# Batch by batch: the norms, transposes and copies ahead of the second mixture of experts

## The reference

```python
x = x + jnp.tanh(g_xattn[2]) * _L2_xattn_ref(_layernorm(x, axis=-1), ctx_2048, ...)
x = x + jnp.tanh(g_ffn[2]) * _L2_ffn_ref(_layernorm(x, axis=-1), ...)

def _L2_ffn_ref(x, router_logits, gating_einsum, linear, per_expert_scale, router_scale):
    var = jnp.mean(jnp.square(x.astype(jnp.float32)), axis=-1, keepdims=True)
    router_input = x * jax.lax.rsqrt(var + 1e-06) * root_size * router_scale
    logits = jnp.einsum('gsd,de->gse', router_input, router_logits)      # 8 experts
    _, choices = jax.lax.approx_max_k(logits, k=2)
    # softmax weights of the two chosen; each expert: gelu(x w_gate) * (x w_up), then its linear
```

## Time and profile before

| | us |
|---|---|
| median of 3 runs | 1482.22 |
| lowest, highest | 1480.7, 1485.71 |
| the profiled execution, its time | 1479.47 |
| the profiled execution, its span | 1477.8 |
| PE busy | 1335.5 (90%) |
| DVE busy | 1031.1 (70%) |
| ACT busy | 795.1 (54%) |
| POOL busy | 668.1 (45%) |
| mean granted clock of PE | 0.963 |

### The profile page before, as it was taken

One profiled execution on the slowest core, in us unless ns is written; L12 is line 12 of the kernel. 1 busy time (PEld: TensorE's weight loads), 2 busy tenths in 40 slices (PEclk: granted clock), 3 DMA queues, 4 the chain that ended last, 5 costly groups with the idle time before them and its releaser, 6 DMA issues.

```text
span 1477.8 us, 23050 instructions
## 1 busy us (share of the span) xinstructions
PE 1335.5 (90%) x7138; PEld 1093.5 (74%) x7138; DVE 1031.1 (70%) x2191; ACT 795.1 (54%) x1978; POOL 668.1 (45%) x675
## 2 busy tenths in 40 slices
PE   5987999998899999977899889999989899999994
PEld 3545888886487877766788567888877788888884
DVE  7786556555687777657754757878787877786654
ACT  6744222222566666653222467767777677787342
POOL 1010454543343434324632145556557676766443
PEclk9997999998999999997999999999999999999997
DMA  6221545562200000010110199000120000105283
GB/s 217 93 93 52 173 160 176 161 181 61 79 8 23 8 16 1 1 43 15 43 43 28 43 253 293 7 1 15 30 94 29 30 30 29 58 17 193 76 285 112
DMA packets 66705, 120.80 MB, mean 82 GB/s; under 512 B 6644, under 2 KB 35976, under 8 KB 65579
## 3 DMA queue, kind: packets, MB, share of 16 engines
q1 hardware_dynamic: 64347, 115.33, 24.8%
q0 software_dynamic: 2256, 4.22, 0.8%
HBM read 82.53 MB, written 38.96 MB: 82 GB/s over the span
## 4 chain that ended last, share of the span: by engine, by line
PE 61%; DVE 17%; issue 7%; ACT 6%; DMA 5%; POOL 4%; SPq 1%; POOLq 0%; DVEq 0%; ACTq 0%
PE ps L1479 8%; PE ps L1452 8%; PE ps L1430 7%; PE ps L1351 6%; PE ps L1497 6%; PE ps L1295 5%; PE ps L1462 4%; PE ps L1157 4%; PE ps L1441 3%; DMA w<-in_l1f_w 3%; PE ps L1365 3%; PE ps L1311 2%; POOL urs L910 2%; DVE usum L2847 2%; DVE nmax L2872 1%
## 5 line engine op out<-in xcount | busy, mean ns | idle before, releaser
L917 POOL TENSOR_TENSOR probs<-probs,prec 128x512 f32<-128x512 f32 x192 | 202.1, 1053 | 324.2 <-DVE prec L2879 323.9
L2068 ACT ACTIVATE probs<-ps,nmax 128x256 f32<-128x256 f32 x384 | 178.6, 471 | 217.9 <-DVE nmax L2872 217.6
L1479 PE MATMUL ps<-probs_t,v_tok 128*128 128x256 f32 x768 | 200.7, 385 | 0.2 <-ACT ob L2087 0.2
L1452 PE MATMUL ps<-k_feat,q_feat 128*128 128x256 f32 x768 | 198.6, 381 | 1.9 <-ACT q_feat L2059 1.9
L910 POOL TENSOR_TENSOR urs<-uve,neg_half 128x4 f32<-128x4 f32 x136 | 136.9, 1007 | 56.4 <-DVE uve L2848 45.8
L2872 DVE TENSOR_REDUCE nmax<-ps 128x2 f32<-128x512 f32 x192 | 131.6, 686 | 31.4 <-PE ps L1452 28.4
L1452 PEld LDWEIGHTS ps<-k_feat,q_feat 128*128 128x128 f32 x768 | 137.4, 191 | 16.0 <-issue 2.7
L1462 PEld LDWEIGHTS ps<-ident,probs 128*128 128x128 f32 x768 | 93.8, 142 | 64.8 <-issue 36.6
L1479 PEld LDWEIGHTS ps<-probs_t,v_tok 128*128 128x128 f32 x768 | 133.0, 193 | 10.8 <-ACT probs_t L2077 0.4
L1462 PE MATMUL ps<-ident,probs 128*128 128x128 f32 x768 | 117.7, 276 | 20.9 <-ACT probs_t L2077 20.5
L2077 ACT ACTIVATE probs_t<-ps 128x512 f32<-128x512 f32 x192 | 115.1, 599 | 3.2 <-PE ps L1462 3.2
(11 more groups left out here) (405 smaller groups left out, 3626.4 us busy)
## 6 DMA issues: line engine op xcount, KB each, us to landing
rows_in<-zero_rows SPq DMA_DIRECT2D x3, 5160.0 KB, 40.9
tile_w<-in_l3f_w SPq DMA_DIRECT2D x21, 385.5 KB, 7.3
w<-in_l1f_w SPq DMA_DIRECT2D x24, 256.0 KB, 6.6
spread_w<-we_dram SPq DMA_DIRECT2D x16, 384.0 KB, 3.8
kv_cross<-kv_out SPq DMA_DIRECT2D x20, 256.0 KB, 2.2
kv_first<-kv_out SPq DMA_DIRECT2D x16, 256.0 KB, 2.0
spread_w<-we_dram SPq DMA_DIRECT2D x16, 256.0 KB, 3.9
w<-in_l2f_w SPq DMA_DIRECT2D x8, 512.0 KB
```

The source lines that it names most:

```text
L917: pool.tensor_tensor(p3, p3, spread(prec[g % 3][:, :], [P, TB, S]), ALU.mult)\
L1452: mm = pe.matmul(ps[g % 2][:, j * S:(j + 1) * S], q_feat[:, h, j * P:(j + 1) * P], k_feat[:, kv, :], start=True, stop=True)
L1479: mm = pe.matmul(ps[6][:, 0:S], v_tok[:, tb, kv * P:(kv + 1) * P], probs_t[g % 2][:, tb, :], start=tb == 0, stop=tb == TB - 1)
L2068: ins = act_e.activation(probs[g % 4][:, j, :], ps[g % 2][:, j * S:(j + 1) * S], ACT.Exp, bias=nmax[g % 3][:, j:j + 1], accum_out=psums[g ...
```

## The change

The work on the normalised x is cut into batches, and that for batches 0, 1 and 2 is put into the hooks of the last slots of `l2x`:

- DVE: statistics in slots 54, 55, 56, the shift in 57, 58, 59, the rests `h_lo` in 66, 67, 68.
- POOL: three roots of 2 columns in slot 57.
- ACT: the centred and scaled `h_tok` in slots 58, 60, 61, the copy to `h_feat` in 63, 64, 65, the rounded copy `h_hi` in 65, 66, 67.
- PE: four identity products per batch in slots 62, 63, 64.

Only batch 3 is done after the attention, in the same steps. `h_tok` is now made by ACT, from shift and scale, and no longer by DVE. The router's mean square isn't taken from moments of `h_tok`, but worked out from variance and scale of x (`rstd`² · variance), and its root (L896 in the changed kernel) stands on POOL behind the first weight split. PE does the logits of the first three batches, then eight products with the identity whose result nobody reads (`keep_clock`), and then batch 3. ACT's one copy of the output weights is cut into four, in units 2 to 5 of the experts.

```diff
@@ POOL @@
-            run(attention(L2X))
-            ln_scale()
-            ln_scale()
-            split_weights(L2F, lambda: low_output(wsets[1]["o"]))
+            def scales_second(t):
+                if t == 57:
+                    part_scales(3)
+            run(attention(L2X, scales_second))
+            part_scales(1)
+            split_weights(L2F, lambda: low_output(wsets[1]["o"]), root_mean_square)
...
                     first(0, 0)
+                    first_split()
                     first(0, 1)
...
+            def root_mean_square():
+                n_ln[0] += B
+                pool.wait_ge(ln_var, n_ln[0])
+                pool.tensor_tensor(rrec[:, :], var_eps[:, :], neg_half[:, 0:NT], ALU.pow).then_inc(ln_rstd, B)
@@ PE @@
-            run(attention(L2X, begin_late(FIRST_LN, h_tok)))
-            turn(h_tok, h_ready, (1, 2))
-            feat_ready()
-            logits(wg2, 8)
+            def toward_l2f(t):
+                first_late(t)
+                if t in (62, 63, 64):
+                    b = t - 62
...
+                    turn_part(SECOND_LN, b, h_tok, quantised, (SECOND_LN - 1) * B + b + 1, ps[2 + b % 2])
+            run(attention(L2X, toward_l2f))
+            pe.wait_ge(part_out, SECOND_LN * B + 3)
+            logits(wg2, 8, 0, 3 * TB)
+            keep_clock(8, 6)
+            turn_part(SECOND_LN, 3, h_tok, quantised, SECOND_LN * B, ps[5])
+            pe.wait_ge(part_out, SECOND_LN * B + 4)
+            logits(wg2, 8, 3 * TB, NT)
@@ ACT @@
                 late(t)
+                if t in (58, 60, 61):
+                    centre_part(SECOND_LN, (58, 60, 61).index(t), h_tok)
+                if t in (63, 64, 65):
+                    second_copy(t - 63, ps[2 + (t - 63) % 2])
+                if t in (65, 66, 67):
...
+                    second_high(b, part(h_feat, b))
...
-            copy_turned(h_feat, h_hi)
+            centre_part(SECOND_LN, 3, h_tok)
+            second_copy(3, ps[5])
+            second_high(3, two(ps[5]))
             router(8, ACT.Exp, 2)
-            act_e.wait_ge(layer_done, 5)
-            act_e.wait_ge(lw["wo_in"], 16)
-            act_e.activation(w_high["o"][:, :, :], wsets[1]["o"][:, :, :], ACT.Copy)\
-                .then_inc(lw["wo_hi"], 1)
-            experts(L2F)
+            def high_output(u):
...
+                if 2 <= u < 6:
+                    heads = slice(4 * (u - 2), 4 * (u - 1))
+                    copied = act_e.activation(w_high["o"][:, heads, :], wsets[1]["o"][:, heads, :], ACT.Copy)
+                    if u == 5:
+                        copied.then_inc(lw["wo_hi"], 1)
+            experts(L2F, high_output)
@@ DVE @@
-                if t == 62:
-                    variance(x_tok, 0)
+                if t in (54, 55, 56):
+                    part_moments(SECOND_LN, t - 54)
+                if t in (57, 58, 59):
+                    part_shift(SECOND_LN, t - 57)
+                if t in (66, 67, 68):
+                    second_low(t - 66)
...
-            layernorm(x_tok, 1)
-            v.wait_ge(turned_out, 4 * 1)
-            v.wait_ge(h_ready, 2)
-            for half in range(2):
-                moments(h_tok, half)
-            split_base[0] = 0
-            split_h()
-            link(v.tensor_tensor(rsum[:, :], mv[:, :, 0], mv[:, :, 0], ALU.mult))
-            v.scalar_tensor_tensor(var_eps[:, :], rsum[:, :], 1e-6, mv[:, :, 1], ALU.add, ALU.add)\
-                .then_inc(ln_var, 2)
...
+            part_moments(SECOND_LN, 3)
+            part_shift(SECOND_LN, 3)
+            link(v.tensor_tensor(rsum[:, :], rstd[:, :], rstd[:, :], ALU.mult))
+            link(v.tensor_tensor(rsum[:, :], rsum[:, :], mv[:, :, 1], ALU.mult))
+            v.tensor_scalar(var_eps[:, :], rsum[:, :], 1e-6, None, ALU.add).then_inc(ln_var, B)
+            second_low(3)
+            v.wait_ge(ln_rstd, (SECOND_LN + 2) * B)
```

More of the change, by code:

```diff
@@ L1266, in _, with logits @@
                 fourth(b)
-            def logits(w, E):
-                for t in range(NT):
+            def logits(w, E, first, last):
+                for t in range(first, last):
                     for kb in range(KB):
@@ L1720, in _ @@
             st = Steps(act_e, act_step)
-            jobs = [0]
-            def copy_turned(feat, high=None):
-                for c in range(4):
-                    act_e.wait_ge(turned, 4 * jobs[0] + c + 1)
-                    part = (slice(None), c % 2, slice((c // 2) * HALF, (c // 2 + 1) * HALF))
-                    if high is not None:
-                        act_e.activation(high[part], ps[c][:, :], ACT.Copy).then_inc(h_hi_ready, 1)
-                    act_e.activation(feat[part], ps[c][:, :], ACT.Copy).then_inc(turned_out, 1)
-                jobs[0] += 1
             def block(t2, g):
@@ L1946, in router, with experts @@
                 act_e.activation(ex[:, :, 0:E], lgx[:, :, 0:E], func).then_inc(exp_ready, 1)
-            def experts(f):
+            def experts(f, beside):
                 s = fs[f.name]
@@ L2119, in _, with second_copy, second_high @@
             late = begin_late(FIRST_LN, h_tok)
+            def second_copy(b, bank):
+                act_e.wait_ge(part_turned, SECOND_LN * B + b + 1)
+                act_e.activation(part(h_feat, b), two(bank), ACT.Copy).then_inc(part_out, 1)
+            def second_high(b, source):
+                act_e.activation(part(h_hi, b), source, ACT.Copy).then_inc(h_hi_ready, 1)
             def high_self(t):
                 late(t)
+                if t in (58, 60, 61):
[3 more added lines that the diff above has]
+                if t in (65, 66, 67):
+                    b = t - 65
+                    act_e.wait_ge(part_out, SECOND_LN * B + b + 1)
+                    second_high(b, part(h_feat, b))
                 p = t - 56
@@ L2606, in top2_mask, with second_low @@
                 link(v.tensor_tensor(msk[:, :, 0:E], msk[:, :, 0:E], lgx[:, :, 0:E], ALU.add))
-            splits = [4]
-            def split_h():
-                for c in range(4):
-                    splits[0] += 1
-                    v.wait_ge(h_hi_ready, splits[0])
-                    v.wait_ge(turned_out, split_base[0] + c + 1)
-                    part = (slice(None), c % 2, slice((c // 2) * HALF, (c // 2 + 1) * HALF))
-                    v.tensor_tensor(h_lo[part], h_feat[part], h_hi[part].bitcast(F32), ALU.subtract)\
-                        .then_inc(h_split, 1)
-            split_base = [0]
+            def second_low(b):
+                v.wait_ge(h_hi_ready, B + b + 1)
+                v.wait_ge(part_out, SECOND_LN * B + b + 1)
+                here = (slice(None), slice(None), slice(b * S, (b + 1) * S))
+                v.tensor_tensor(h_lo[here], h_feat[here], h_hi[here].bitcast(F32), ALU.subtract).then_inc(h_split, 1)
             def experts(f):
@@ L2993, in _ @@
             part_moments(LAST_LN, 2)
-            n_ln[0] += B
             def residual(b):
```

79 lines of the change are left out of this document (18 added, 61 removed).

## The result

| | before | after |
|---|---|---|
| median, us | 1479.54 (6 runs, 1475.29 to 1485.71) | 1467.61 (6 runs, 1465.12 to 1470.28) |
| the profiled execution, its time | 1479.47 | 1466.27 |
| its span | 1477.8 | 1464.6 |
| mean granted clock of PE | 0.963 | 0.971 |

The ratio after to before is 0.9931, interval [0.9905, 0.9956]: the changed kernel is 10 us faster (6.5 to 14). The forecast was 1477, range 1470.5 to 1484. Part of that is the base: the three runs of before that the forecast started from had a median of 1482.22; six, these three among them, have 1479.54.

A forecast was written before the change was run, and what follows sets the result against it. PE was taken as the bound, busy 90%, with time to win only in its waits or low clock, here from `l2x` to the experts. -10.7 + 3.4 + 2.0 = -5.3 from the median 1482.22 gave 1477 us, range 1470.5 to 1484.

The forecast's parts named there:

- term B: Last slots of `l2x`: work added there costs 3.4 us, bounded by -0.4 (all hidden) and 10.2 (all on the path).
- term C: PE at the first expert units: after a 2.9 us wait for `gated` its clock falls, costing 2.0 us.
- term A: Passage from `l2x` to the experts `L2F`: the first `gated` product comes earlier, at 676.9, gaining 10.7 us.
- upper bound of 2.0: Router's root of 8 columns on POOL: at most 2.0 us, both old steps together; 1.6 was taken.
- the cover of ACT's copy: ACT's copy of `wo`, quartered in units 2 to 5: 2.1 us of ACT work per unit, hidden behind at least 2.2.
- "mostly paid" step: Last slots of `l2x`: ACT work ahead of `probs_t` is mostly paid; three centred copies, 3.3 us, cost 2.3.
- D, `wo_low`: After the third expert unit: PE's 4.7 us standstill behind POOL's `wo_low` moves along unchanged, 0 us.
- the second: Rival: the last `l2x` slots cover nearly all and PE's clock holds; -9.3 us, 1473 us, chance 0.16.
- The third: Rival: the router's chain is no shorter, POOL blocks DVE for 12.9 us as before; -0.3 us, 1482, chance 0.22.
- the fourth: Rival: longer waits drop PE's clock within the last `l2x` slots; slower by 6.3 us, 1488.5, chance 0.10.

The follow-up runs named there:

- e4: Changed kernel with the router's root on POOL behind both weight splits instead of between them; `x_tok` to `gated` 22.64 us, against 20.11.
- e6: Changed kernel with the router's root on POOL ahead of both weight splits instead of between them; `x_tok` to `gated` 18.86 us, against 20.11.
- e3: Changed kernel with ACT's copy of `wo` whole again, ahead of the experts; `x_tok` to `gated` 20.99 us, against 20.11.
- e1: Kernel before with eight identity products ahead of PE's long wait in the drain; slot 57 to `x_tok` 36.53 us instead of 38.20.
- e9: Changed kernel with one more ACT copy of 1.08 us in slots 59 and 62; slot 57 to `x_tok` 39.82 us, against 39.28.
- e5: Changed kernel with 12 identity products in PE's wait ahead of the third expert unit; refill load 6.51 us behind `gated`, experts 136.2 us, against 137.0.
- e8: Kernel before with only the first weight split moved ahead of the router's root on POOL; `x_tok` to `gated` 31.53 us, against 30.95.
- e11: Kernel before with POOL's `wo_low` in four quarters; experts 130.5 us instead of 136.3, one run 1475.28 us beside a median of 1485.94.

## Why the prediction was wrong in size

The forecast was -5.3 us; the stretches that the change touches gave -9.0. The time came 9.4 us under the 1477 that was forecast: 2.7 of it is the base, 2.3 term B, 1.3 term C, 0.1 term A, and 3 lie outside these stretches. By its own steps:

- **A, the passage: right.** -10.7 forecast, -10.8 measured. Its pieces: first expert matmul 9.4 us behind `x_tok` (666.1 - 656.66 = 9.4 forecast); `h_lo` held by `w_lo`; the chain from the root's end to the mark 9.3 us (9.2 forecast). The root of 8 columns took 2.08 us there, a little above the upper bound of 2.0, and 1.64 in e4 and e6, the value taken; the order of POOL and DVE absorbed the difference, since `h_lo` was held and not in between. e4 shows that the mark hangs on the root, e3 that the cover of ACT's copy was indeed thin, 0.9 us.
- **B, the last slots: the step that failed most.** 3.4 forecast, 1.1 measured. The forecast's sum for the added work was 3.4, that work measured 2.7 once the clock is held (e1). What it left out is the other 1.6: the fall of the clock in the drain, which costs the kernel before 1.7 us (e1). It had read the 2.15 us wait and the 1.67 us product behind it, and used them only to price term C. It didn't ask whether the transposes that it put into these very slots would fill that wait. By the clock of 1.00 there they did, and a cost of before went. The "mostly paid" step was too strict as well, by e9, though the slots with a centred copy weren't tried alone.
- **C, the clock behind the longer wait: right in kind, its size not fixed.** 2.0 forecast, +0.7 in the column of the experts, in two profiles of the changed kernel; in e9, whose experts are the same code, it would be +2.5. The wait came (3.69 us, 2.9 forecast), the clock fell to 0.52, and by e5 and its neighbours that costs 1.5 to 2.9 us at the refill load, of which 0.8 was left at `h_late`. But it is no pure cost of the change: e1, e8 and e11 have the passage of before or nearly so, and it fell there too. The one profile of before happened to be the cheap case, and a term was worked out as a difference to it.
- **D, `wo_low`: right.** 4.8 us against 4.7, in its place.
- **The base.** The median of three runs was 2.7 us above that of six. With -9.0 the first base would give 1473, inside the range; with the later one 1470.5, its edge. The measured 1467.6 has 3 us more, which is within the scatter of the outer columns; its cause isn't shown.

Of the rivals, the second (slots nearly free, -9.3 us) came nearest in size. Its two reasons were half right: the slots were nearly free, but the clock did fall behind the wait. The third fell with e4 and the chain of 9.3 us; the fourth with the clock of 1.00 in the drain.

## What to carry to other kernels

When work is moved into slots of an engine whose clock falls in waits, price both sides: what the work costs there, and what the wait that it fills had cost. A long GpSimd operation that reads SBUF is worth cutting where a short VectorE step on the path can start under it; cutting one of 9.5 us into four took 5.8 us off the experts of the kernel before and 6.7 off the changed kernel's. And judge a change of under 1% by stretches that repeat to a few tenths of a us, not by the difference of two spans whose untouched parts scatter by 7 us and more; and profile the base more than once, since its clock can fall in one execution and not in another.

## What was not expected of the hardware

- Not only DVE steps with two tensors are held by POOL: the normalising of e8, one tensor and scalars per partition, went from 2.83 to 6.51 us.
- POOL's root of 8 columns took 1.64 us in e4 and e6 and 2.08 in the changed kernel, where it stood beside the end of DVE's `h_lo`; of 2 columns it took 0.70.
- PE's clock stayed up behind a wait of 1.90 us with transposes shortly before it, and fell behind one of 2.15 us; behind 1.86 us in e1 (0.81 in the stretch around), 2.08 in e11 (0.74) and 1.97 in e6 (0.60) it fell too, with no such work before. So the length of the wait alone doesn't tell; what does isn't shown.
